# Moving a LayerNorm apply from ScalarE to VectorE, and the statistics ahead of a weight sum

## What is computed

```python
def _L0_attn_ref(x, W, b):
    params = jnp.einsum('btc,dc->btd', x, W) + b        # 2048 -> 4096
    gates, values = jnp.split(params, 2, axis=-1)
    gates, values = jax.nn.sigmoid(gates), jnp.tanh(values)
    _, hidden = jax.lax.associative_scan(_scan_op, (gates, values), axis=1)
    return hidden                                       # h[t] = g[t]*h[t-1] + v[t]
def _L0_ffn_ref(x, w_fc, w_proj):                       # hidden width 5120
    h = jnp.square(jax.nn.relu(x @ ternarize_weight(w_fc).T))
    return h @ ternarize_weight(w_proj).T
x = x + _layernorm(_L0_attn_ref(_layernorm(x), W, b))
x = x + _layernorm(_L0_ffn_ref(_layernorm(x), w_fc, w_proj))
```

## Time and profile before

| what | us |
|---|---|
| median of 2 runs | 5681.58 (5677.77 to 5685.39) |
| profiled execution, whole | 5580.75 |
| its span (core 6, the slowest of 8: 5513.3 to 5579.1) | 5579.1 |
| scan stage in it, 277.6 to 1761.7 | 1484.1 |
| TensorE busy (share of the span) | 3703.9 (66%) |
| VectorE busy | 1507.3 (27%) |
| ScalarE busy | 1225.1 (22%) |

### The profile page before, as it was taken

One profiled execution on the slowest core, in us unless ns is written; L12 is line 12 of the kernel. 1 busy time (PEld: TensorE's weight loads), 2 busy tenths in 40 slices (PEclk: granted clock), 3 DMA queues, 4 the chain that ended last, 5 costly groups with the idle time before them and its releaser, 6 DMA issues.

```text
span 5579.1 us, 61463 instructions; the slowest of 8 cores (5513.3 to 5579.1 us)
## 1 busy us (share of the span) xinstructions
PE 3703.9 (66%) x21046; PEld 2184.6 (39%) x21254; DVE 1507.3 (27%) x2942; ACT 1225.1 (22%) x2768; POOL 255.7 (5%) x476
## 2 busy tenths in 40 slices
PE   0066574757574344443389697896978969879697
PEld 0056464646464222222134343343443434434343
DVE  0033333343434566666500201102011020110202
ACT  0022222222221232332331120311203112031120
POOL 0001101010101000000000000000000000000000
PEclk9988787878787555555599798897989979889898
DMA  9722324232315777776574655746657466574653
GB/s 110 154 99 82 123 70 134 69 122 83 125 64 179 238 248 238 247 243 222 189 176 153 195 152 162 181 155 192 155 162 180 156 188 153 169 177 153 162 155 130
DMA packets 931677, 884.97 MB, mean 159 GB/s; under 512 B 813488, under 2 KB 813616, under 8 KB 879152
## 3 DMA queue, kind: packets, MB, share of 16 engines
q1 hardware_dynamic: 826800, 469.93, 30.4%
q0 software_dynamic: 49536, 276.85, 16.3%
q10 hardware_dynamic: 55040, 134.24, 7.7%
HBM read 704.76 MB, written 176.16 MB: 158 GB/s over the span
## 4 chain that ended last, share of the span: by engine, by line
PE 60%; DMA 12%; DVE 11%; issue 6%; ACT 5%; another core or an unknown queue 3%; SPq 2%; ACTq 1%; DVEq 0%; POOL 0%; POOLq 0%
PE ps_pj L963 20%; PE ps_fc L951 19%; PE ps_par L439 15%; DMA x_sb<-x 4%; PE ps_bf L613 3%; DMA wslab<-wfc 3%; DVE st6c L46 2%; DMA wslab<-wpj 2%; PE ps_yT L974 2%; DMA sfc_sb<-sfcT_t 2%; ACT stage_fc L581 1%; ACT stage_pj L581 1%; DVE st6a L46 1%; DVE out_sb L841 1%
## 5 line engine op out<-in xcount | busy, mean ns | idle before, releaser
L951 PE MATMUL ps_fc<-xn1T_sb,sfc_sb 128*128 128x512 bf16 x5016 | 1129.1, 386 | 269.7 <-DMA sfc_sb<-sfcT_t 220.3
L439 PE MATMUL ps_par<-xnT_sb,wt_sb 128*128 128x256 bf16 x8192 | 940.2, 278 | 493.2 <-ACT g_sb L397 468.7
L963 PE MATMUL ps_pj<-hfc_sb,spj_sb 128*128 128x512 bf16 x5016 | 1100.9, 379 | 22.4 <-ACT hfc_sb L882 15.3
L439 PEld LDWEIGHTS ps_par<-xnT_sb,wt_sb 128*128 128x128 bf16 x8192 | 813.7, 100 | 607.8 <-issue 499.3
L951 PEld LDWEIGHTS ps_fc<-xn1T_sb,sfc_sb 128*128 128x128 bf16 x5120 | 506.3, 99 | 891.2 <-issue 308.5
L963 PEld LDWEIGHTS ps_pj<-hfc_sb,spj_sb 128*128 128x128 bf16 x5120 | 500.3, 98 | 623.0 <-issue 21.6
L46 DVE BATCH_NORM_STATS2 st6c<-ps_yT 128x6 f32<-128x512 f32 x128 | 79.7, 685 | 2361.5 <-PE ps_yT L974 2361.5
L613 PE MATMUL ps_bf<-idbf_sb,ssl 128*128 128x128 bf16 x1280 | 294.6, 265 | 358.5 <-DVE ssl L687 141.9
L878 ACT ACTIVATE r_sb<-ps_fc,am_fc 128x512 f32<-128x512 f32 x320 | 219.8, 687 | 678.3 <-PE ps_fc L951 674.3
L613 PEld LDWEIGHTS ps_bf<-idbf_sb,ssl 128*128 128x128 bf16 x1280 | 133.9, 105 | 522.5 <-issue 478.6
L890 ACT COPY y_sb<-ps_pj 128x512 f32<-128x512 f32 x128 | 74.9, 585 | 1041.3 <-PE ps_pj L963 1041.3
(11 more groups left out here) (77 smaller groups left out, 1842.7 us busy)
## 6 DMA issues: line engine op xcount, KB each, us to landing
sfc_sb<-sfcT_t SPq DMA_DIRECT2D x320, 512.0 KB, 4.6
spj_sb<-spjT_t SPq DMA_DIRECT2D x128, 1280.0 KB, 5.8
wslab<-wfc POOLq DMA_DIRECT2D x160, 256.0 KB, 4.5
wslab<-wpj POOLq DMA_DIRECT2D x160, 256.0 KB, 3.8
wslab<-wfc ACTq DMA_DIRECT2D x160, 256.0 KB, 5.1
wslab<-wpj ACTq DMA_DIRECT2D x160, 256.0 KB, 4.1
x_sb<-x SPq DMA_DIRECT2D x16, 2048.0 KB, 7.9
h_t<-h_sb POOLq DMA_DIRECT2D x32, 1024.0 KB, 7.7
```

The lines of the kernel that those rows point to most:

```text
L439: ins = tensor.matmul(pp[:, 0:CH1], wt_sb[:, ct, col0:col0 + 128], xnT_sb[:, k % 2, ct, :], start=(ct == 0), stop=(ct == NC - 1))
L951: ins = tensor.matmul(ps_fc[gh % 2][:, 0:CH2], sfc_sb[:, gh % 3, ct, :], xn1T_sb[:, q % 2, ct, :], start=(ct == 0), stop=(ct == NC - 1))
L963: ins = tensor.matmul(ps_pj[gc % 2][:, 0:CH2], spj_sb[:, gc % 2, ht, :], hfc_sb[:, ht, :], start=(ht == 0), stop=(ht == NH - 1))
```

## The change

VectorE applies the LayerNorm itself: `stats_seg(k)` loses the computation of `nmrs1`, waits until chunk k-1's transposes have been made (`p_xt`), and then writes `xnb_sb` with two `tensor_scalar` instructions of 128x2048 (subtract the mean, multiply by the reciprocal deviation; f32 in, bf16 out), which also signal `s_nm4`. ScalarE keeps only the square root of `ln1_seg`. And VectorE's order becomes: stats(0), stats(1); then for k = 1 to 15: scan(k-1), stats(k+1) where there is one, abs(k-1). Between scan(k-1) and scan(k) there stand now stats(k+1) with its apply and then abs(k-1).

```diff
@@ stats_seg
                         vector.wait_ge(vs4, vcnt)
+                        _w(vector, p_xt, NC * TT1 * k)
                         for tt in range(TT1):
-                            ins = vector.scalar_tensor_tensor(
-                                out=nmrs1[:, tt:tt + 1], in0=mv1[:, tt, 0:1],
-                                scalar=-1.0, in1=rs1[:, tt:tt + 1],
-                                op0=ALU.mult, op1=ALU.mult)
-                        ins.then_inc(v_lnb, 1)
+                            ins = vector.tensor_scalar(
+                                out=xnb_sb[:, 0, tt, :], in0=x_sb[:, 0, tt, :],
+                                scalar1=mv1[:, tt, 0:1], scalar2=rs1[:, tt:tt + 1],
+                                op0=ALU.subtract, op1=ALU.mult)
+                            ins.then_inc(s_nm4, 1)
                         return vcnt
@@ order on VectorE
+                    vcnt = stats_seg(vector, 1, vcnt)
                     for k in range(1, NCH):
-                        vcnt = stats_seg(vector, k, vcnt)
                         scan_seg(vector, k - 1, xk=k)
+                        if k + 1 < NCH:
+                            vcnt = stats_seg(vector, k + 1, vcnt)
                         abs_seg(vector, k - 1)
@@ ln1_seg on ScalarE
                         scalar.sqrt(sd1[:, 0:TT1],
                                     veps1[:, 0:TT1]).then_inc(s_sq4, 1)
-                        scalar.wait_ge(v_lnb, k + 1)
-                        _w(scalar, p_xt, NC * TT1 * k)
-                        for tt in range(TT1):
-                            scalar.activation(
-                                out=xnb_sb[:, 0, tt, :],
-                                in_=x_sb[:, 0, tt, :], func=AF.Identity,
-                                bias=nmrs1[:, tt:tt + 1],
-                                scale=rs1[:, tt:tt + 1]).then_inc(s_nm4, 1)
```

## The result

| what | before | after |
|---|---|---|
| undisturbed runs, us | 5579 to 5604 | 5333, 5334, and one of 5381 |
| ratio after to before | | 0.9547, 95% interval 0.9506 to 0.9588 |
| end of the scan stage, mean over cores | 1746.1 | 1500.5 |
| weight sums from first to last in each chunk, summed over 16 chunks, mean over cores | 385.9 | 460.2 |
| TensorE waiting for gate tiles, mean over cores | 458.0 | 200.0 |

A forecast was written before the change was run, and what follows sets the result against it. The scan stage was taken as TensorE's work plus one long stall per chunk, 33.0 us at each of 14 boundaries. Saving 14 x 18.1 + 6.8 = 260 us, taken off the runs' median, gave 5421.6 us; range 5340 to 5510.

The forecast's parts named there:

- Stall one: TensorE's wait at a chunk's start, behind statistics and square root that now start right after the scan: 3.2 us.
- The apply: VectorE's two new tensor_scalar instructions, from f32 rows with output type taken as free: 1.29 us each, bound 2.68.
- E+10.5: Forecast end of VectorE's apply at boundary 8, with E = 1027.5, the end of scan(7).
- The moved load, c = 4: Load of x now ahead of the weight sums; c is its cost per boundary, 4 us, the middle of 0 and 7.9.
- the upper bound: The load of x displaces the piece loads fully: c = 7.9 us, the time it alone takes to land.
- The wait for h_t: The scan's wait for h_t after the weight sums, no longer covered by the statistics: 1.9 us.
- The rival in which it takes the gain back: Late h_t writes replace the removed wait: saving 1.7 us per boundary, 31 in all, 5651 us; chance 0.07.
- Stall two: TensorE's wait before group 16, behind the weight sums: 9.0+c us at boundary 8, 6.0+c with the mean boundary's sums.
- Restart, r = 2.2: Slowness of TensorE's matmuls in group 16 after stall two: 2.2 us taken, bounds 0 and 2.9.
- The clock rival: TensorE never regains the upper clock level between the two stalls: 18.4 us lost per boundary, 5932 us; chance 0.04.
- The start, 6.8 us: Chunk 0's apply and stats(1) shrink: 1.9 us at the first and about 4.9 us at the second.
- The sum: Whole saving: 14 boundaries at 18.1 us plus 6.8 us at the start, 260 us.

The follow-up runs named there:

- e3: The changed kernel with the load of x waiting until the chunk's weight sums are done; 5269 and 5279 us, ratio 0.9448.
- e6: The changed kernel with the load of x cut in two, 1 MB before the weight sums and 1 MB behind them; 5302 to 5312 us, ratio 0.9501.
- e1: The kernel before with only VectorE's new order, the apply staying on ScalarE; 5303, 5310 and 5351 us, ratio 0.9533.
- e4: The changed kernel with the weight sums put between its scans and the first h_t write behind the 14th piece load; 5173 and 5174 us.
- e5: e4 with the next statistics and their square root put in mid-scan, and weight sums ending with pair 13; 5066 to 5071 us, ratio 0.9074.

## Why the prediction was right, step by step

- **Stall one, 3.2 us**: measured 3.22 us at most boundaries (3.01 to 3.51), as the sum of rows gave it.
- **The apply, 1.29 us each**: a little low.

```profile
L266 DVE TENSOR_SCALAR xnb_sb<-x_sb,mv,rs 128x2048 bf16<-128x2048 f32 x32 | 41.6, 1344 | 2.8 <-DVE rs L260 2.7
```

  1344 ns. Two rows of different sizes always lie on one line, so they could not show that the output type is free; the guess came out within 58 ns of the f32 row. No run shows what these 58 ns are: the output type and the second scalar both differ from that row. At chunk 8 the sums start at E+10.9 instead of E+10.5, but over the 14 boundaries the mean is 10.5, as added up.
- **The moved load, c = 4**: the term that was mis-sized. It costs 5.3 us at 13 boundaries (against e3, and against cores 0 to 3 of before alike), 69 us where 14 x 4 = 56 were put down. The middle between two bounds was not the best choice: 42% idle DMA time looked like room, but none of it was, for even the 1 MB of e6 cost its full share. A row of before would have served better. Where the engines are full, behind the sums,

```profile
1051.30:1060.00 8.70, 0.00 (x0) 0.00 (x0) 6.56 (x12) 0.00 (x0) 3.23 (x7) 0.50 0.97 353
```

  they move 353 GB/s at a share of 0.97, and 2.1 MB at this rate are 5.9 us, an estimate some 10% above what was measured. The whole 7.9 us of the load's landing, the upper bound, was too high. The DMA share over these sums is 0.73 (907.4 to 939.7 us), above the 0.58 of before as forecast. The Trainium skill (DMA: Bandwidth & Descriptors, Queues, rings and completion order) describes a service of the queues in turn. The trace agrees in so far as the first piece of chunk 8's boundary, issued 1.07 us behind the load of x, lands at 915.52, before x at 916.85. That the pieces lose in proportion to the bytes in front does not tell this order from another: whatever keeps the engines at work in any order costs them the same bytes.
- **The wait for h_t, 1.9 us**: 31.1 us over 15 scan segments, 2.1 us each. The rival in which it takes the gain back did not come; landing was 5.9 to 10.6 us.
- **Stall two, 9.0+c for this boundary, 6+c on average**: 14.88 us at chunk 8, 3.72 (the last, without a load of x) to 14.9 elsewhere. **Restart, r = 2.2**: the 128 matmuls behind it took 16.0 us in the mean of the 14, against 14.14, so 1.9.
- **The clock rival**: wrong in its strong form. The next 128 matmuls behind a slow block take 14.14 us, the full rate, each time, and the clock of the stage rose from 0.84 to 0.91 (core 3).
- **The start, 6.8 us**: on cores 0 to 3 group 16 of chunk 0 begins 9.6 us earlier than before, at 308.6.
- **The sum**: on cores 0 to 3 of both kernels the stage ends 250.8 us earlier, against 260. The time from one group 16 to the next falls from 94.3 to 77.0 us in the mean of the 14 boundaries, 17.3 each where 18.1 were put down. The load (13 us), h_t (3) and the last boundary with the tail (1) are 17 us less than added up, the milder restart (4) and the start (3) 7 us more; that gives 250, so within a microsecond or so nothing is left over. The forecast came out close partly because these misses point both ways.
- **The basis.** I took the saving off a median 101 us above the profiled execution. The runs since show that the latter, 5580.8, stands among the undisturbed ones of before (5579 to 5604), so the forecast as a time, 5421.6, was on the wrong footing, and 5333 lies 7 us below the stated range of 5340 to 5510. The ratio is the fair comparison: 0.954 predicted (0.953 if 260 is taken off 5580.8), 0.9547 measured.

What the prediction did not see, though its own sum held it: the two parts work against each other. Its terms put the apply on VectorE in front of the sums (2.6 us) and ScalarE's 4.1 us only in front of stall one, which stall two swallows. Reading that off would have said that the order alone is better, as e1 then showed.

## What to carry to other kernels

When work that nobody waits for stands in an in-order queue in front of work on which another engine's buffers depend, move it behind, and better still cut it up and put it into the queue's own gaps: the first gave 5% (e1), the second (e4, with the h_t write ahead) another 3% to the changed kernel, the statistics in mid-scan (e5) 2% more. Where an engine has two stalls in a period and the end of the second does not hang on the first, only the second counts, so relief in front of the first is worth nothing and may cost; ask for each instruction which stall it stands in front of. Put a transfer that is moved in front of a DMA-paced stream at its bytes over the rate at which the engines run full (here 10% above the measured price), not at what is left of their idle share.

## What the runs showed of the hardware that I had not expected

A stall of 3.2 us of TensorE is enough, sometimes, to cost clock. At the first stall of the changed kernel the 64 matmuls behind it took 7.15 us in 6 of 14 chunks and 8.4 to 10.1 us in the other 8, with nearly the same stall ahead of them (3.0 to 3.5 us) and the same work; over cores 0 to 3 it was 36 of 56. Two such chunks, on core 3, the first at a granted clock of 1.00, the second at 0.71:

```profile
666.75 7.15 PE L434 MATMUL ps_par<-xnT_sb,wt_sb 128*128 128x256 bf16 x64 [3.22 <-ACT g_sb L392]
...
744.67 9.89 PE L434 MATMUL ps_par<-xnT_sb,wt_sb 128*128 128x256 bf16 x64 [3.22 <-ACT g_sb L392]
```

No run here explains which of the chunks are slow. With 5.0 us (e4) all 14 were slow, from 8.6 to 9.8 us, and the penalty is then as large as behind 35 us. A stall thus costs more than its own length: in e4 5.0 us and 2 more. The other surprise is how little the kind of transfer matters: loads of x by one queue and writes of h_t by another delay the pieces by nearly the same, 2.6 and 2.7 us per MB.
